# Extra products on the identity for TensorE in a four-layer transformer kernel

## The reference, cut to what matters

```
x = x + L0_attn(layernorm(x))   # rotary, 16 heads of 16, causal, 1024 keys
x = x + L0_ffn(layernorm(x))    # silu(x W1') * (x W3'), Hadamard transform, W2
x = x + L1_attn(layernorm(x))   # 16 heads, causal
x = x + L1_ffn(layernorm(x))    # silu gate * up, 2 of every 4 kept, down
x = x + L2_attn(layernorm(x))   # gated linear recurrence along the rows
x = x + L2_ffn(layernorm(x))    # router, 2 of 8 experts, and a shared expert
x = x + L3_attn(layernorm(x))   # the sequence axis has length 1: each row sees one key
x = x + L3_ffn(layernorm(x))    # ternary weights, gate * up, rms norm, down
```

## Time and profile before

| | us |
|---|---|
| three runs | 963.4, 967.69, 969.59 |
| their median | 967.69 |
| the profiled execution: device time | 962.79 |
| its span, first to last instruction | 961.0 |
| its mean granted clock of TensorE | 0.901 |
| busy: PE / PEld / DVE / ACT / POOL | 797.6 / 513.8 / 624.4 / 387.0 / 153.4 |

### The profile page before, as it was taken

One profiled execution on the slowest core, in us unless ns is written; L12 is line 12 of the kernel. 1 busy time (PEld: TensorE's weight loads), 2 busy tenths in 40 slices (PEclk: granted clock), 3 DMA queues, 4 the chain that ended last, 5 costly groups with the idle time before them and its releaser, 6 DMA issues. The chain is left out here.

```text
span 961.0 us, 12407 instructions
## 1 busy us (share of the span) xinstructions
PE 797.6 (83%) x4306; PEld 513.8 (53%) x4306; DVE 624.4 (65%) x1318; ACT 387.0 (40%) x655; POOL 153.4 (16%) x208
## 2 busy tenths in 40 slices
PE   6256899987899678999986896669999999478796
PEld 5143344325688553334255786555556666266575
DVE  6887888808774689788346977452267771265764
ACT  3141457683521423666746432541122222043543
POOL 1800121120020001112210000105112221100143
PEclk9666899999899787999998997769999999888798
DMA  6227300000000472200007000993201110310000
GB/s 206 93 81 217 103 2 1 3 2 1 1 1 1 147 246 84 67 3 2 2 1 127 1 1 1 326 375 113 66 28 45 45 45 27 109 45 1 1 23 22
DMA packets 49554, 63.96 MB, mean 67 GB/s; under 512 B 12534, under 2 KB 34806, under 8 KB 49494
## 3 DMA queue, kind: packets, MB, share of 16 engines
q1 hardware_dynamic: 47622, 58.05, 19.7%
q0 software_dynamic: 1872, 5.13, 1.5%
HBM read 50.30 MB, written 15.51 MB: 68 GB/s over the span
## 5 line engine op out<-in xcount | busy, mean ns | idle before, releaser
L806 DVE TENSOR_REDUCE at1mx<-at1ps_s 128x1 f32<-128x512 f32 (+3 forms) x152 | 90.7, 655 | 17.5 <-PE at1ps_s L708 10.4
L806 DVE TENSOR_REDUCE at0mx<-at0ps_s 128x1 f32<-128x512 f32 (+3 forms) x152 | 90.7, 655 | 17.0 <-PE at0ps_s L708 10.0
L786 ACT ACTIVATE at1probs<-at1ps_e 128x1024 f32<-128x1024 f32 (+3 forms) x96 | 73.8, 809 | 45.9 <-PE at1ps_e L729 45.5
L786 ACT ACTIVATE at0probs<-at0ps_e 128x1024 f32<-128x1024 f32 (+3 forms) x96 | 73.8, 809 | 45.5 <-PE at0ps_e L729 45.2
L1070 PE MATMUL f2ps<-gu_raw,f2xT_b 128*128 x184 | 82.9, 593 | 1.0 <-ACT f2xT_b L1145 1.0
L1163 ACT ACTIVATE f2sg<-f2ps 128x512 f32<-128x512 f32 x31 | 18.5, 598 | 134.3 <-PE f2ps L1070 100.9
L705 PE MATMUL at0ps_s<-ks,qs 96*128 96x512 bf16 (+3 forms) x192 | 58.1, 364 | 6.8 <-DMA ks<-scratch 5.3
L705 PE MATMUL at1ps_s<-ks,qs 96*128 96x512 bf16 (+3 forms) x192 | 58.0, 363 | 6.0 <-DMA ks<-scratch 4.4
L1239 DVE TENSOR_TENSOR f2h<-f2sg,f2ps 128x512 f32<-128x512 f32 x31 | 21.3, 686 | 61.6 <-ACT f2sg L1163 42.1
L1070 PEld LDWEIGHTS f2ps<-gu_raw,f2xT_b 128*128 128x128 f32 x184 | 34.8, 190 | 35.5 <-issue 34.4
L729 PE MATMUL at1ps_e<-qs,ks 99*128 99x512 bf16 (+3 forms) x192 | 46.7, 339 | 4.1 <-ACT at1probs L786 2.3
(11 more groups left out here) (400 smaller groups left out, 1772.1 us busy)
## 6 DMA issues: line engine op xcount, KB each, us to landing
gu_raw<-in_L_ffn_w_gate_up SPq DMA_DIRECT2D x8, 1024.0 KB, 12.4
scratch<-parts SPq DMA_DIRECT2D x8, 768.0 KB, 3.8
qs<-scratch SPq DMA_DIRECT2D x48, 128.0 KB, 2.8
ks<-scratch SPq DMA_DIRECT2D x48, 128.0 KB, 2.8
dn_raw<-in_L_ffn_w_down SPq DMA_DIRECT2D x8, 512.0 KB, 12.2
f2x_in<-slots_in SPq DMA_DIRECT2D x23, 129.0 KB, 2.0
slots_in<-in_c_empty SPq DMA_DIRECT2D x1, 2944.0 KB, 17.2
traw<-in_L_ffn_w_gate_up SPq DMA_DIRECT2D x1, 2048.0 KB, 11.6
```

The source lines that it names most:

```text
L786: act.activation(probs[:, slots(v), 0:n], ps_e[:, v % SCORE_PAIRS, :, 0:n], ACT.Exp, scale=HD ** -0.5)\
L806: dve.tensor_reduce(mx[:, p % 2, lo // CH, j:j + heads, t], rows_of, AX.X, ALU.max).then_inc(s_red, 1)
```

## The change

A helper `keep_busy` issues a given number of products of the bf16 identity (weights) with the identity repeated four times (512 columns) into a PSUM bank that isn't in use; nobody reads them and nobody waits for them. They are placed:

- in `norm_stage` without `ident_ready` (n2, n4, n5, n6): 9 ahead of the transpositions, 8 behind;
- in `HalfNorm.turn`, first half (n1, n3, n7): 9 ahead, 8 behind, into `ps_u[:, 1, :]`;
- in each attention: 6 at the stage's start, and one ahead of each of the 39 entries of `ORDER` before the first values, into `ps_v`;
- at the end of the single-key stage: a wait for the sixth copy, then 12.

That is 7 x 17 + 2 x 45 + 12 = 221 products. No other instruction is removed or moved.

```diff
--- before.py
+++ after.py
@@ -70,6 +70,13 @@
     pool.tensor_copy(parts[0][:], raw).then_inc(chain_sem, 1)
     pool.wait_ge(chain_sem, 1)
     pool.tensor_tensor(parts[1][:], raw, parts[0][:].bitcast(F32), ALU.subtract)
+
+
+def keep_busy(pe, m, bank, count):
+
+    for _ in range(count):
+        pe.matmul(bank.rearrange("p (a n) -> p a n", n=P), m.identb[:], m.identb[:].unsqueeze(1).to_broadcast([P, CH // P, P]),
+                  start=True, stop=True)
 
 
 def sem(nc, own, name):
@@ -242,6 +249,8 @@
         def _(pe):
             if ident_ready is not None:
                 pe.wait_ge(*ident_ready)
+            else:
+                keep_busy(pe, m, ps[:, 7, :], 9)
             for half in range(2):
                 for j in range(CH // P):
                     t = half * (CH // P) + j
@@ -253,6 +262,8 @@
                         ins = pe.transpose(ps[:, half * KD + k, j * P:j * P + P], xn[:, t, k * P:k * P + P], m.ident[:])
                         if j == CH // P - 1:
                             ins.then_inc(tr_ready, 1)
+            if ident_ready is None:
+                keep_busy(pe, m, ps[:, 7, :], 8)
 
 
 @stage
@@ -642,6 +653,7 @@
 
 ORDER = order_of_products()
 MAXIMA_BY = [sum(kind == "max" for kind, _ in ITEMS[:i + 1]) for i in range(len(ITEMS))]
+FIRST_VALUES = ORDER.index(("values", 0))
 ROWS_BEFORE = [sum(kind == "scores" for kind, _ in ORDER[:ORDER.index(("item", ITEMS.index(("rows", p))))]) for p in range(len(PHASES))]
 
 
@@ -747,8 +759,11 @@
                                     start=(kt == 0), stop=(kt == (qc + 1) * TILES - 1))
                 ins.then_inc(pv_done, 1)
 
+            keep_busy(pe, m, ps_v[:], 6)
             pe.wait_ge(m.stacked_ones, 16)
-            for kind, n in ORDER:
+            for place_in_order, (kind, n) in enumerate(ORDER):
+                if place_in_order < FIRST_VALUES:
+                    keep_busy(pe, m, ps_v[:], 1)
                 if kind == "scores":
                     scores(n)
                 elif kind == "values":
@@ -1294,7 +1309,7 @@
 class HalfNorm:
 
 
-    def __init__(self, nc, own, tmp, tag, room):
+    def __init__(self, nc, own, tmp, tag, room, spare):
         names = ("_sums", "_stats", "_std", "_inv", "_shift", "_xn_v", "_xn_a", "_tr", "_high", "_ready")
         (self.sums, self.stats, self.std_s, self.inv, self.shift_s, self.xn_v, self.xn_a, self.turned, self.high_s,
          self.ready) = (sem(nc, own, tag + x) for x in names)
@@ -1307,7 +1322,7 @@
         self.std, self.rstd = sb("std", [P, T]), sb("rstd", [P, T])
         self.shift = sb("shift", [P, T // 2])
         self.warm = sb("warm", [P, 1])
-        self.room = room
+        self.room, self.spare = room, spare
 
     def tiles(self, half):
         return range(half * T // 2, (half + 1) * T // 2)
@@ -1350,6 +1365,8 @@
     def turn(self, pe, m, half):
         if half:
             pe.wait_ge(self.ready, KD)
+        else:
+            keep_busy(pe, m, self.spare, 9)
         for j, t in enumerate(self.tiles(half)):
             if t % 2:
                 pe.wait_ge(self.xn_a, t // 2 + 1)
@@ -1358,6 +1375,8 @@
             for k in range(KD):
                 ins = pe.transpose(self.room[:, k, j * P:j * P + P], self.xn[:, t, k * P:k * P + P], m.ident[:])
         ins.then_inc(self.turned, 1)
+        if not half:
+            keep_busy(pe, m, self.spare, 8)
 
     def high(self, act, m, half):
         act.wait_ge(self.turned, half + 1)
@@ -1404,7 +1423,7 @@
         ps_u = tmp.enter_context(nc.psum_tensor(tag + "ps_u", [P, 2, CH], F32))
         ps_o = tmp.enter_context(nc.psum_tensor(tag + "ps_o", [P, OB, TC, D], F32))
         ps_q = tmp.enter_context(nc.psum_tensor(tag + "ps_q", [P, CH], F32)) if sums else None
-        nm = HalfNorm(nc, ctx, tmp, norm, ps_o[:, OB - 1].rearrange("p (k t) d -> p k (t d)", k=KD))
+        nm = HalfNorm(nc, ctx, tmp, norm, ps_o[:, OB - 1].rearrange("p (k t) d -> p k (t d)", k=KD), ps_u[:, 1, :])
         block = tmp.enter_context(nc.Block())
 
         def piece(a, f):
@@ -1687,7 +1706,7 @@
         ps_g = tmp.enter_context(nc.psum_tensor(tag + "ps_g", [P, 2, CH], F32))
         ps_u = tmp.enter_context(nc.psum_tensor(tag + "ps_u", [P, 2, CH], F32))
         ps_o = tmp.enter_context(nc.psum_tensor(tag + "ps_o", [P, 2, TC, D], F32))
-        nm = HalfNorm(nc, ctx, tmp, norm, ps_o[:, 1].rearrange("p (k t) d -> p k (t d)", k=KD))
+        nm = HalfNorm(nc, ctx, tmp, norm, ps_o[:, 1].rearrange("p (k t) d -> p k (t d)", k=KD), ps_u[:, 1, :])
         block = tmp.enter_context(nc.Block())
         PAIRS = {(0, 1): 0, (0, 2): 1, (1, 2): 3, (0, 3): 2, (1, 3): 4, (2, 3): 5}
 
@@ -1977,6 +1996,8 @@
                     for i, src in enumerate(blocks[t][0]):
                         ins = pe.transpose(ps_b[:, t % 2, i * P:i * P + P], src, m.identb[:])
                     ins.then_inc(turned, 1)
+            pe.wait_ge(copied, len(blocks))
+            keep_busy(pe, m, ps_b[:, 0, :].bitcast(F32), 12)
 
         @block.scalar
         def _(act):
```

## The result

Ten runs of the changed kernel have a median of 961.45 us (960.52 to 964.7), ten of the kernel before 968.33 (963.4 to 971.04). The ratio is 0.9942 with a 95% interval of 0.9926 to 0.9957: 0.6% faster, inside one per cent of no change. The profiled execution took 961.3 us, its span is 959.5, its mean granted clock 0.943 where before had 0.901.

What follows compares the result with a forecast made beforehand. TensorE was taken to be the bound where busy at clock 0.50, mostly behind normalisations, in the attentions' first twenty us, expert stage and o3. 962.8 less 12.0, attentions 0, gives 950.8; plus 1.7 towards the median, 952.5 us; range 941 to 963.

Steps and rivals of the forecast that it cites:

- I take 0, nearest to the warm case with its start cold: Attentions: their fillers change the time by 0 us, with bounds of -1.3 and +14 per attention.
- TensorE idles for the stacks' DMAs, and the 6 fillers bring only 1.3 to 2.6 us of work: Attention's start: begins cold, so each maximum costs 0.39 us more until the clock is up, some 2 to 3 us.
- So warm, the fillers fit between VectorE's reads: Attentions: TensorE's warm 0.48 us per maximum with filler, against VectorE's 0.57, keeps the clock; VectorE's waits shrink, at best 1.3 us.
- The base: Whole kernel: starts from 962.8 us, 4.9 below the median 967.69, and carries 1.7 of the 4.9 over.
- The normalisations and single keys: Stages outside the attentions: warm starts gain 12.6 us, less 2 x 0.3 for n5 and n6, so 12.0.
- its ceiling of 3.1: f3: half of 4.77 us busy at 0.50, 2.4, plus 0.7 for ScalarE's wait; 2.5 of it expected.
- half: Recurrence: 2.9 us of pause stays ahead of it, so half of its 2.4 us ceiling comes, 1.2.
- most of the router's gain and little of the rest: Expert stage: enters warm, clock falls during the router or just behind; 2.9 us of the 5.8 ceiling.
- A later engine takes the gain: Rival, f0, f1 and s1: VectorE or the stacks' DMAs absorb their 4.5 us, giving 957; chance 0.07.
- The clock falls anyway in the 2-us pauses: Rival, normalisations: a third of each ceiling instead of two thirds, some 5 us, 957.8 or 960; chance 0.2.
- Slower: the fillers run at the lower level in the attentions: Rival: identity products hold no clock, +14 us in each attention, 38 in all, giving 1001; chance 0.05.
- the same or shorter waits for TensorE: Sign that the forecast is right: VectorE's group L806 keeps the same or shorter waits for TensorE; no size.

Runs made afterwards that it cites:

- run 2: The changed kernel without any filler in the attentions (6 and 39 gone from each): 953.93 us, once more 954.33.
- run 3: The kernel before with the attentions' fillers alone (2 x 45): 975.3 us, ratio 1.0069.
- run 8: The changed kernel with 16 fillers at the split stages' ends and, in the attentions, only those ahead of the first 20 entries: 954.42 us.
- run 11: Run 2's kernel plus, per attention, 10 fillers ahead of phase 2's maxima, 3 ahead of phase 1's first scores, and 16 at each split stage's end: 953.09 us.
- run 13: Run 11's kernel plus one filler ahead of each of an attention's first 20 entries: 953.57 us, ratio 0.9848.
- run 17: Run 13's kernel plus 8 fillers in o1 behind the first two transpositions: 948.93 us, ratio 0.9818.
- run 1: The changed kernel without the 6 fillers at each attention's start, the 39 kept: 959.42 us, ratio 0.9912.
- run 9: The changed kernel less the later 19 of the 39 fillers in each attention, the 6 and first 20 kept: 958.67 us.
- before again: The kernel before, run and profiled once more with no edit: 967.21 us.
- run 16: Run 2's kernel with each filler product of 512 columns replaced by four transpositions of the identity: 953.95 us.
- run 5: The changed kernel without the 39 fillers in each attention, the 6 at the start kept: 954.38 us.
- run 6: Run 2's kernel with only the 9 fillers in front at the normalisations, without the eight behind and the single keys': 963.35 us.

## Why the prediction was wrong

**The step that failed: the attentions, "I take 0, nearest to the warm case with its start cold".** The bounds, -1.3 to +14 each, held; the value was mis-sized. Between run 2's kernel and the changed one the profiles differ by 7.6 us, the medians by 7.5. Of the 7.6, 2.1 and 2.4 lie ahead of the first scores of at0 and at1, 0.4 and 0.6 in the attentions, 2.7 in o1; the other rows come to -0.5. The first 4.5 are the step's own error, shown below. The 2.7 are not explained: o1 has the same instructions in both kernels, the level fell 2.1 us behind its first product in the changed kernel (the line at 496.50) and held in run 2's, and in run 3, with the same 90 fillers, o1 took 15.5 as in run 2. Three things in the step were read wrongly or left out.

- *"TensorE idles for the stacks' DMAs, and the 6 fillers bring only 1.3 to 2.6 us of work".* It idles, but nearly all of it lies ahead of the meeting at the split stage's end, not behind it. When TensorE enters the attention at 79.54 (its 4.86 us of idle time end with the meeting), it is 20.2 us behind s0's first product; in the kernel before, the first score came at 20.7. Half a us was free, and seven fillers at 0.43 us stand in it. What hid them in my sum wasn't there. The same work placed ahead of the meeting (runs 8, 11, 13, 17) delays next to nothing: 20.7 to 20.9 us from s0 to at0's first score and 21.4 to 22.2 from s1 to at1's, where run 2 has 21.0 and 21.8, and both are at the full level. Leaving out the six alone (run 1) gives the delay back, and the cold start then costs maxima.
- *"So warm, the fillers fit between VectorE's reads".* True for the first 20: the stretches show 1.00, VectorE is busy 9.12 of ten us where it had about 8.7. I sized a maximum against a filler (0.48 against 0.57) and left it at "TensorE is behind by up to 1" where the five scores lie. Between the first scores and the first values TensorE has maxima, scores and 19 fillers, is busy without a break, and VectorE waits for it 1.0 us in three pieces. Run 9 took the 19 away: maximum 33 of at1 came 1.5 us sooner, its last exponential 1.9. In the changed kernel this loss eats what the warm start had gained: its 45th maximum stands 0.4 (at0) and 0.0 us (at1) later behind the first score than in run 2, so for the time behind the first score 0 was near.
- *What a warm start is worth in an attention.* The level at 1.00 instead of 0.5 to 0.7 in those twenty us gave 1.1 to 1.5 us of maxima, since VectorE sets the pace. This I had said ("at best 1.3 us"), and it was about right: 21.6 us to maximum 33 in run 9's at1, 22.7 and 23.1 in run 2.

**The base.** 962.8 was an execution without the stall marked "remote"; from the shared products to n6 it took 195.79 us and every later profile, of either kernel, 197.9 to 200.3. I carried 1.7 of the 4.9 us between profile and median; with "before again" (967.2) as the base, the same 12.0 would give 955. What the stall is stays open, and no run was made for it.

**The normalisations and single keys: 12.0 forecast, about 13.5 by profile (before again against run 2), 13 to 14 by medians.** The sum was near, its terms less so (those measured add up to 15.1; 1.6 of it is lost ahead of n1 and in n6):

| | forecast | measured |
|---|---|---|
| f0 | 1.2 | 0.9 |
| f1 | 1.3 | 1.4 |
| s1 | 2.0 | 2.4 |
| recurrence | 1.2 | -0.1 |
| n5, router, shared products (2.9 less 0.3) | 2.6 | 3.8 |
| o3 | 1.5 | 0.4 |
| f3, with n7 | 2.5 | 4.6 |
| o1, not forecast | 0 | 1.7 |

The router did halve (6.8 us to 3.6 between its first product and the shared ones), where only the transposition's row had spoken for it (start to start these are 0.213 us apart at 0.50 and 0.109 at 1.00; the prediction's 0.23 and 0.13 hold the last one's tail), and in these profiles the clock held through it: the forecast had left nothing for what lies behind. The recurrence gained nothing here, as the level fell in the 3.7 us of idle time ahead of it (changed kernel) or 0.7 us behind its first product (run 2). That is one of two outcomes: of the 14 profiles with these fillers, five have 30.3 us or more from n4 to n5 and 12.0 from n5 to the shared products, the other nine 27.6 to 29.5 and 14.6 to 14.8. In run 17 the recurrence's first products stand 0.23 us apart behind 2.6 us of idle time, and the router takes 4.6. So "half" and "most of the router's gain and little of the rest" were each right in some executions; from n4 to the shared products the two together gave 2.9 in run 2's profile. f3 gained more than its ceiling of 3.1, as a later fall near its end is gone in some profiles (58.41 us from f3's first product to the end in run 2, 59.9 in others). o1 and o3 take 15.5 or 17 to 18, and 10.2 or 11.8, in kernels whose instructions there are the same: where the level falls after a thin stretch differs from profile to profile, so single rows of this table are worth 1.5 us, the recurrence's and the router's nearly 3, and the sum more than its parts.

**The rivals.** "A later engine takes the gain" didn't come: s1's 2.4 us went to at1 whole. "The clock falls anyway in the 2-us pauses" came at n1 (the eight behind it cold, 3.28 us, f0 0.3 us late) and n5's front, not as the rule. "Slower: the fillers run at the lower level in the attentions" had the right place and, but for the seven at each start, the wrong state: the rest ran at 1.00 and cost all the same.

**What was to be seen:** L1491 0.23 us apart in f3, the router at 3.7, VectorE's first wait at 2.69, the clock above 0.93: all as forecast. That VectorE's group keeps "the same or shorter waits for TensorE" failed, at maxima 31 to 33 only (counted from 0). I had named a wrong sign too coarse to catch it (a wait at each maximum).

## What to carry to other kernels

Filler products pay where TensorE waits for another engine and then has products alone on the path; they belong ahead of a meeting of the engines or inside the very wait, never behind it in front of the first due instruction. Where another engine sets the pace, the clock is worth little (here 1.1 to 1.5 us where TensorE's work shrank by an estimated eight, 17.3 to 9.5 in the prediction's sum), and a filler costs as soon as TensorE's list has no gap; count the list's busy time with the fillers entry by entry, most of all where a second kind of work joins it. Test each group of fillers by itself: here one group gave back half of what the others had gained, and the sum hid both.

## What the runs showed of the hardware

- Transpositions hold and raise TensorE's level as products do: in run 16 36 and 32 of them gave the router 1.00 and the kernel the same time (953.95 and 953.93), and the stretch 845.7 to 849.2 of the earlier trace rows said so before. The Trainium skill, "TensorE: Matmul & The Clock Gate", Part 4 (PE-mode transpose), says that the full clock doesn't engage for them, since they don't count as busy in the same way; these runs go against it, and the measurement decides. They hold for transpositions as `pe.transpose` issues them here, which the rows list as MATMUL; whether the page's transpose mode is set in them isn't shown.
- Products on the identity hold and raise it too, though most of what they multiply is zeros: at0's first score in the changed kernel is at 1.00 behind seven of them that began at 0.50, and in run 17 sixteen ahead of the meeting and twenty behind it give at0 1.00 over its first ten us, where run 2 has a mean of 0.67. They stand 0.216 us apart at 1.00 (2.10 us for nine ahead of n7) and 0.43 at 0.50.
- Products of 8 columns with weights of their own halve with the level too: 32 in 6.97 us at 0.50 and in 3.71 at 1.00.
- In the middle of an attention TensorE waits 0.4 to 1.0 us at a time, for the maxima's banks and for the rows. In run 2's profile the level was down behind that (0.78 over the eight us), in run 8's for ten us (0.51), and with thirteen fillers in those waits it stayed at 1.00 there in all 14 attentions that have them. Why it didn't fall there in both attentions of run 5 and in at0 of runs 3 and 6, with the same instructions in these waits as elsewhere, stays open.
